# A graph network on one core: edge chunks dealt by degree, sums scattered to DRAM in node order, counts added in DRAM cells

## What is computed

```python
# graph attention, used twice: 8 heads, then 1 head
fs = x @ Ws + bs;  fd = x @ Wd + bd
e = leaky_relu(fs[src] + fd[dst], 0.2)
logits = einsum('ehd,hd->eh', e, attn)
alpha = softmax of logits over the edges of one dst
out = elu(segment_sum(alpha * fs[src], dst))
# whole network
h = relu(ln(x));  h = ln(gat8(h) + h);  x = x + ln(gat1(h))
h = relu(ln(x))
# relational layer: mean over the edges of one type into a node
h1 = sum_r mean_r(h)[n] @ W_rel[r] + h @ W_root + b
# convolution with counts of edges
out = segment_sum(xw[src] * dinv[src] * dinv[dst], dst) + xw * dinv**2 + b,  xw = h1 @ W_gcn
x = x + out
```

## Time and profile before

| what | value |
|---|---|
| runs | 3333.24 us median of 3 (3331.61 to 3335.16) |
| span of the profiled execution | 3343.9 us, 10.7 over that median |
| busy: PE, DVE, ACT, POOL | 2854.4, 2290.3, 1702.4, 1620.6 us |
| same, share of the span | 85%, 68%, 51%, 48% |
| DMA | 546.00 MB, mean 163 GB/s |

### The profile page before, as it was taken

The page is one execution under the profiler, slowest core; times in us unless marked ns, Lnnn a source line. Parts: engine busy times, 40 slices in busy tenths (PEclk is TensorE's granted clock), DMA queues, the critical chain, the costliest instruction groups (busy, mean ns, idle before and its releaser), DMA issues. The chain is left out here.

```text
span 3343.9 us, 59649 instructions
## 1 busy us (share of the span) xinstructions
PE 2854.4 (85%) x13556; PEld 2139.5 (64%) x13557; DVE 2290.3 (68%) x4351; ACT 1702.4 (51%) x5372; POOL 1620.6 (48%) x2067
## 2 busy tenths in 40 slices
PE   5885888888789799998668999999999976777799
PEld 3442454454455455554348999999999974555598
DVE  6535889889767788887565555555555447888743
ACT  0004889899722133332545566555665566777300
POOL 4666566565446555554114545544544445555201
PEclk9897999999999899999789999999999998999899
DMA  4235344444511555555228777777776747666412
GB/s 141 84 81 159 121 135 126 124 134 124 170 46 44 157 167 170 171 170 175 89 95 263 243 242 245 242 237 237 247 241 219 222 144 230 203 210 208 119 34 65
DMA packets 175008, 546.00 MB, mean 163 GB/s; under 512 B 55331, under 2 KB 56343, under 8 KB 174723
## 3 DMA queue, kind: packets, MB, share of 16 engines
q0 software_dynamic: 82000, 370.33, 35.3%
q1 hardware_dynamic: 70596, 122.50, 11.8%
q10 hardware_dynamic: 22304, 52.11, 5.4%
HBM read 461.31 MB, written 83.81 MB: 163 GB/s over the span
## 5 line engine op out<-in xcount | busy, mean ns | idle before, releaser
L2189 PE MATMUL pO<-wh,gT 128*128 128x384 f32 x3264 | 867.1, 339 | 17.6 <-ACT gT L2140 15.6
L805 POOL DMA_INDIRECT row<-fs_d,rec x400 | 455.9, 1140 | 389.6 <-PE pA L1330 157.5
L2189 PEld LDWEIGHTS pO<-wh,gT 128*128 128x128 f32 x3264 | 594.4, 189 | 26.4 <-ACT gT L2140 23.0
L2189 PE MATMUL pO<-wl,gT 128*128 128x384 f32 x1632 | 547.5, 335 | 0.0
L2203 DVE TENSOR_SCALAR cntge<-pT 128x768 int32<-128x768 int32 x137 | 131.2, 958 | 427.2 <-ACT gT L2140 223.1
L1038 ACT ACTIVATE sj<-sj 128x96 f32<-128x96 f32 x1176 | 312.9, 268 | 78.7 <-DVE sj L1155 78.5
L2189 PEld LDWEIGHTS pO<-wl,gT 128*128 128x128 f32 x1632 | 308.3, 189 | 0.0
L2140 ACT ACTIVATE gT<-cntge 128x256 fp32r<-128x256 f32 x822 | 292.9, 410 | 28.1 <-DVE cntge L2206 4.0
L805 POOL DMA_INDIRECT row<-y_d,rec x200 | 204.1, 1020 | 171.6 <-PE pR L2335 113.5
L1077 PE MATMUL pS<-row,ident 128*128 128x384 f32 x400 | 176.2, 524 | 128.3 <-DVE sj L1155 80.9
L2335 PE MATMUL pR<-row,share 128*128 128x384 f32 x384 | 165.7, 582 | 120.6 <-issue 65.0
(11 more groups left out here) (386 smaller groups left out, 5983.8 us busy)
## 6 DMA issues: line engine op xcount, KB each, us to landing
fdt<-in_L_gnn_W_rel_dram SPq DMA_DIRECT2D x170, 384.0 KB
startrow<-seen_d ACTq DMA_DIRECT2D x141, 320.0 KB
raw<-in_L_gnn_W_rel_dram SPq DMA_DIRECT2D x34, 384.0 KB
row<-fs_d,rec POOLq DMA_INDIRECT x400
kept_d<-fdt SPq DMA_DIRECT2D x10, 384.0 KB
kept<-kept_d SPq DMA_DIRECT2D x10, 384.0 KB
fs_d<-of SPq DMA_DIRECT2D x9, 388.0 KB
fd_d<-of SPq DMA_DIRECT2D x9, 388.0 KB
```

What stands on the lines that cost most here:

```text
L805: pool.indirect_dma_start(b["row"][u][:, j, :].bitcast(words), None, table, bass.IndirectOffsetOnAxis(ap=b["rec"][u][:, 2 * j + field:2 * ...
L2189: last = pe.matmul(pO[:, q, 0:HALF], gT[:, c, half, :].bitcast(F32R), w[:, c, lo:up].bitcast(F32R), start=c == 0 and k == 0, stop=c == KC ...
```

## The change

- Nodes are dealt to the 128 partitions in a serpentine by degree rank. Each partition has a stream of chunks of four edges, its nodes one behind another; a group is the next chunk of every stream. 44 groups (11 turns) hold all chunks of these inputs. DVE makes 16 words for each of 64 groups in one block (row of records, node, edges left, target, whether first or last chunk), and SP stores them; the packed table of tiles and `sum_tiles` are gone, as are `perm`, `permc` and `degr`.
- A group's destination row is gathered by POOL with its four source rows (`own_of`). Running sums are in a ring of four slots, `sum0` to `sum3`. POOL scatters each group's sums to `first_d`, `second_d` or `ysum_d` in node order (`sums_out`); partitions whose chunk is not the node's last have a target of NP or above, which the bounds check drops. Before a slot's target is overwritten, `sum_free` waits for the scatter that used it last. The scatter of group u - 1 is issued behind the fetches of group u + 2.
- The joins load and store tiles in node order by SP. In the first join SP also clears `counts_d` (21 stores) and `ge_d`'s first column. Single attention stores each group's comparison with the types to `ge_d`.
- In the second join POOL works out the weights of all edges of 48 groups (EARLY = 48) in eight parts of six groups, writes them into the group words, and does one further group in a loop that also counts its edges.
- In the relation stage POOL adds ones into the cells of `counts_d` with three accumulating scatters (`tally`) in each of 64 pairs (COUNTED = 64), each waiting for the one before.
- The y stage has no comparisons, transposes or counts: ACT makes two shares from the words, PE multiplies two rows, DVE adds. The convolution loads sums and counts from DRAM; its last store is SP's.

The core of the diff:

```diff
-        groups_d = dram("groups_d", (MAX_TURNS * U + U - 1, P, S * 2), I32)
+        groups_d = dram("groups_d", (P, GROUPS, WORDS), I32)
...
+        first_d = dram("first_d", (2 * NP, W), F32)
+        second_d = dram("second_d", (2 * NP, W2), F32)
+        ysum_d = dram("ysum_d", (2 * NP, D), F32)
+        ge_d = dram("ge_d", (P, 1 + GROUPS, S * (RELS + 1)), BF16)
+        rcnt_d = dram("rcnt_d", (NP, RELS), F32)
+        counts_d = dram("counts_d", ((1 + NP) * NP, 1), F32)
...
+                    v.link(dve.tensor_tensor_scan(chunk_end[:], chunks[:], chunks[:], 0.0, ALU.add, ALU.max))
...
+                    with dve.Fori(0, blocks) as k:
+                        w = Steps(dve, dve_step, k * BLOCK_STEPS + v.base)
+                        w.wait()
+                        w.link(dve.tensor_tensor(begun[:], over(grow[:], 2, shape), over(chunk_from[:], 1, shape), ALU.is_ge))
+                        for f in range(5):
+                            w.link(dve.tensor_tensor(part[:], begun[:], over(rise[:, f, :], 1, shape), ALU.mult))
+                            w.link(dve.tensor_reduce(now[:, f, :], part[:], X, ALU.add))
...
+        def sum_free(eng, b, i, off):
+
+            eng.wait_ge(b["sum_out"][off % U], i * 16 + 16 * (off // U + (off % U == U - 1)))
+
+        def open_sums(pool, b):
+
+            pool.iota(b["to"][U - 1][:], [[1, 1]], base=NP, channel_multiplier=1,
+                      allow_small_or_imprecise_dtypes=True).then_inc(b["to_ok"][U - 1], 1)
+            pool.wait_ge(b["to_ok"][U - 1], 1)
+
+        def keep_target(pool, b, i, off):
+
+            u = off % U
+            sum_free(pool, b, i, off)
+            n = off // U + 1 + (u == U - 1)
+            pool.sem_inc(b["posted"], 1)
+            pool.tensor_copy(b["to"][u][:], word(b, u, R_OUT)).then_inc(b["to_ok"][u], 1)
+            pool.wait_ge(b["to_ok"][u], i + n)
+            pool.sem_inc(b["posted"], 1)
+
+        def sums_out(pool, b, off, table):
+
+            u = off % U
+            pool.indirect_dma_start(table, bass.IndirectOffsetOnAxis(ap=b["to"][u][:], axis=0), b["sum"][u][:], None,
+                                    bounds_check=NP - 1, oob_is_err=False).then_inc(b["sum_out"][u], 16)
...
+            def fetch(i, off):
+                u = off % U
+                pool.wait_ge(b["edges_only"][(u - 1) % U], i * 16 + 16 * ((off - 1) // U + 1))
+                rec_wait(pool, b, i, off)
+                pool.sem_inc(b["posted"], 1)
+                pool.tensor_scalar(edge[:], slot[:].rearrange("p s c -> p (s c)"), word(b, u, R_LEFT, F32), None, ALU.is_lt)\
+                    .then_inc(b["edge_ok"], 1)
+                pool.wait_ge(b["edge_ok"], i * U + (off + 1))
+                pool.sem_inc(b["posted"], 1)
+                edges_only(u)
+                keep_target(pool, b, i, off)
+                pool.wait_ge(b["edges_only"][u], i * 16 + 16 * (off // U + 1))
+                pool.sem_inc(b["posted"], 1)
+                used.wait(pool, i, off - U)
+                pool.sem_inc(b["posted"], 1)
+                rows_of(pool, b, u, table, 0, F32)
+                own_of(pool, b, u, own)
...
+                    record(w % U)
+                    fetch(i, u + ROWS_AHEAD)
+                    for s in done:
+                        s.wait(pool, i, u - 1)
                     pool.sem_inc(b["posted"], 1)
-                    v.wait()
-                    edges_only(w % U)
...
+        def gather_rows(pool, b, table, field, own, out_table, readers, done, words=F32):
+
+            open_sums(pool, b)
+
+            def fetch(i, off):
+                u = off % U
+                rec_wait(pool, b, i, off)
+                pool.sem_inc(b["posted"], 1)
+                keep_target(pool, b, i, off)
+                for used in readers:
+                    used.wait(pool, i, off - U)
+                pool.sem_inc(b["posted"], 1)
+                if own is not None:
+                    own_of(pool, b, u, own)
                 rows_of(pool, b, u, table, field, words)
+
+            for off in range(ROWS_AHEAD):
+                fetch(0, off)
             turns = turns_of(pool)
             with pool.Fori(0, turns) as i:
                 for u in range(U):
-                    w = u + ROWS_AHEAD
-                    pool.wait_ge(b["rec_in"][w % U], i * 16 + 16 * (w // U + 1))
-                    for used in readers:
-                        used.wait(pool, i, w - U)
+                    fetch(i, u + ROWS_AHEAD)
+                    for s in done:
+                        s.wait(pool, i, u - 1)
                     pool.sem_inc(b["posted"], 1)
-                    rows_of(pool, b, w % U, table, field, words)
+                    sums_out(pool, b, u - 1, out_table)
...
-                        def keep(i, off, tile):
-                            total.wait(act, i, off)
-                            act.activation(split(of(acc, tile)), halves(pA[off % 2]), ACT.Copy).then_inc(kept.sem, 1)
+                        def keep(i, off):
+                            whole.wait(act, i, off)
+                            sum_free(act, b, i, off)
+                            act.activation(split(total[off % U][:, 0:D]), halves(pA[off % 2]), ACT.Copy).then_inc(kept.sem, 1)
...
+                        def weigh(v, groups, weight):
+
+                            ge, rel = cge[:, 0:groups], crel[:, 0:groups]
+                            of_node = crow[:, 0:groups, :].unsqueeze(2).to_broadcast([P, groups, S, RELS])
+                            v.link(pool.tensor_tensor(rel, ge[:, :, :, 0:RELS], ge[:, :, :, 1:RELS + 1], ALU.subtract))
+                            v.link(pool.tensor_tensor(rel, rel, of_node, ALU.mult))
+                            n = RELS
+                            while n > 2:
+                                half = n // 2
+                                v.link(pool.tensor_tensor(rel[:, :, :, 0:half], rel[:, :, :, 0:half], rel[:, :, :, n - half:n], ALU.add))
+                                n -= half
...
+                        pool.wait_ge(rec_in, 16)
+                        v = Steps(pool, pool_step)
+                        of_edges(v, EARLY, crec[:], cells[:].rearrange("p (g s) -> p g s", s=S))
+                        pool.wait_ge(rcnt_out, 16)
+                        for part in range(EARLY // PART):
+                            at = part * PART
+                            pool.dma_start(cge[:].rearrange("p g s r -> p g (s r)"), ge_d[:, 1 + at:1 + at + PART, :]).then_inc(cge_in, 16)
+                            for g in range(PART):
+                                pool.indirect_dma_start(crow[:, g, :], None, rcnt_d, bass.IndirectOffsetOnAxis(
+                                    ap=crec[:, at + g, R_NODE:R_NODE + 1], axis=0)).then_inc(crow_in, 16)
+                            pool.wait_ge(crow_in, 16 * (at + PART))
+                            pool.wait_ge(cge_in, 16 * (part + 1))
+                            weigh(v, PART, cweight[:, at:at + PART, :])
+                        pool.dma_start(groups_d[:, 0:EARLY, R_WEIGHT:R_WEIGHT + S].bitcast(F32), cweight[:]).then_inc(weight_out, 16)
...
+                                pool.indirect_dma_start(counts_d, bass.IndirectOffsetOnAxis(ap=ccell[:, j:j + 1], axis=0),
+                                                        ones[:, 0:1], None, compute_op=ALU.add).then_inc(counted, 16)
+                                pool.wait_ge(counted, k * (16 * S) + 16 * (j + 1))
...
+                    def tally(out, j):
+
+                        pool.wait_ge(counted, out * (16 * PER_PAIR) + 16 * j)
+                        pool.sem_inc(posted, 1)
+                        pool.indirect_dma_start(counts_d, bass.IndirectOffsetOnAxis(ap=cindex[:, j:j + 1], axis=0),
+                                                ones[:, 0:1], None, compute_op=ALU.add).then_inc(counted, 16)
+
+                    def pair(v, i, n, out, counting=False):
+
+                        if counting:
+                            pool.wait_ge(counted, out * (16 * PER_PAIR))
+                            pool.sem_inc(posted, 1)
+                            v.link(pool.tensor_copy(cindex[:], cells[:, ds(out * PER_PAIR, PER_PAIR)]))
                         for b in range(PAIR):
                             make_list(v, i, n, b + PAIR)
+                            if counting:
+                                tally(out, 2 * b)
                             t_ok.wait(pool, n, b)
                             pool.sem_inc(posted, 1)
                             fetch(b)
                             if out is not None:
                                 put(v, out, n, b - PAIR)
+                            if counting and b == 0:
+                                tally(out, 1)
 
                     v = Steps(pool, pool_step)
...
+                            dve.scalar_tensor_tensor(out=split(total[u][:]), in0=split(total[(u - 1) % U][:]),
```

(48 more changed lines are left out.)

1080 lines of the change are left out of this document (538 added, 542 removed).

## The result

The changed kernel takes 4121.77 us (median of four, 4110.01 to 4122.28) against 3332.43 of the kernel before: 1.236 times as long, interval 1.234 to 1.238, 789 us slower. The forecast was 3621, with a range that ended at 3790. The side was right, the size was not: the forecast was +288, and +789 was measured.

A forecast was written before the change was run, and what follows sets the result against it. PE was taken to fill most of single attention and the relation stage; in the changed edge stages POOL's chain governs. Terms 4 - 40 + 3 + 108 + 55 + 120 + 38 = +288 gave 3621 us, range 3355 to 3790.

The forecast's parts named there:

- the one fact: Edge stages: POOL's chain per iteration becomes scatter, landing, copy, fetch, because running sums are scattered to DRAM.
- the loop of two groups: Attentions: POOL alternates between two groups; summed steps give 26.4 us in first attention, 25.4 in single attention.
- rival of hidden waits: Whole kernel: fetches two groups ahead and idle time hide POOL's longer chain; -130 us, 3203; chance 0.16.
- only POOL's own work: Whole kernel: landings hide in the edge stages, but weights and tallies cost as forecast; +35 us, 3368; chance 0.18.
- queueing rival: Scatters queue behind rows: landings 3.7 to 5 us, uncovered tally waits +40; +153 us, 3774; chance 0.14.
- Relations, +120: Relation stage: copy and three accumulating scatters raise POOL's pair from 14.28 to 16.2 us; +120 us (0 to +230).
- The landing, 2.0 us: Edge stages: a scatter takes 2.0 us to land, with 0 and 3.7 kept for the range.
- Single attention, +108: Single attention: exposed landing makes 12.7 us a group against PE's 9.1; +108 us (-37 to +150).
- First attention, -40: First attention: start 19 us shorter, 44 groups at 13.2 us against 48 at 12.6; -40 us (-75 to +10).
- Second join, +55: Second join: POOL's eight weight parts, store and serial extra group end at 205 to 210 us against 155; +55 (+10 to +100).
- The recorded +73: Second join: alternative using the skill page's twice-slower two-input GpSimd work, tree 2.3 us a part more; total 3639.
- Y stage, +38: Y stage: POOL's chain of scatter, landing, copy and rows takes 9.4 us a group; +38 us (-50 to +108).

The follow-up runs named there:

- late target: Changed kernel with the target index copied, after its landing wait, behind the row fetches instead of ahead in all edge stages; 3939.6 us against 4122.
- two groups behind: On top of the late target, the scatter of group u-2 instead of u-1 is issued; 3772.2 us, timed again 3763.36, 1.129 times the kernel before.

## Why the prediction was wrong

*What bounds it, and the one fact.* Right. The order scatter, landing, copy, fetch is what sets the y stage and, through the loop of two groups, both attentions. The late target and the two groups behind show it on both sides: 182 and then 167 us. The rival of hidden waits fell; so did that of only POOL's own work. The queueing rival had landings of 3.7 to 5 us; they were 2.3 and 2.6 on the mean, so it fell too in the edge stages, but its waits between tallies came, at 96 us for its 40.

*Relations, +120: the step that failed most,* 230 of the 501 us by which the forecast was short. The term was 11.5 + 4.7 = 16.2 us a pair. Plain scatters without waits give 16.6, of which POOL still waits 1.1 for ACT (69.7 us in the stage), so this much was sized well. Two things were wrong. I priced an accumulating scatter by the marks and the y store, which are plain: it issues in 1.62 us, not 1.1. And I called the waits between tallies covered because a fetch or a list stands between them; at a landing of 4.4 us a list of 2.4 us covers half. Form and waits together are 200 us. The upper end of the term had the waits at 1.7 a pair and no dearer scatter, and so lay at +230 where +350 came.

*The landing, 2.0 us.* Nearly right, though read off one small scatter at the start. It was 2.3 us on the mean in single attention, between 1.3 and 5.3, and 2.6 in the y stage. The 3.7 of the row gather, which I kept as the upper end, was the worse guess.

*Single attention, +108, came +188.* The period is 13.9 instead of 12.6 (43 periods, +55; the loop's own 12.7 would have given 5 us more). The term that failed in the loop is PE's passes, which I priced at 0.33 us from a stage where PE runs without a hole and the clock is 0.98. I had PE starve for 3.5 us a group and did not ask what its passes cost after that. In the round above they took 2.4 us more than that price, and the landings of the scatter and of the rows 0.9 more. And start and end of the stage together grew by 27 us, which I had left unchanged. The last scatter is such an end:

```profile
1843.69 1.00 POOL L884 DMA_INDIRECT second_d<-sum,to  x1 [12.88 <-ACT sum L1372]
...
1855.00 0.38 SPq L1835 DMA_DIRECT2D rden<-second_d  x1
```

From 1844.7 to 1855.0 all engines wait for it, 10.3 us, where in the kernel before the last copy to SBUF was 1.1 us from the next stage. The forecast charged 3 us for this in first attention and nothing here.

*First attention, -40, came +80.* The loop was right in its parts, but 13.2 was the sum of parts at their shortest: 15.5 came, 97 us over 43 periods. PE's 16 passes of sums took 6.9 us (619.22 to 626.09, at a granted clock of 0.50 to begin with, after a wait of 8.2 us) instead of 5.3, and about 7 in most groups. POOL's scatter took 1.5 to 1.7 instead of 1.0, and its index copy 2.0 to the next fetch (637.08 to 639.09) instead of 1.1. The start gave 13 of the 19 us I had booked, and the end cost 19 instead of 3.

*Second join, +55, came +76.* The weights began 27.5 us into the stage for 20 and took 152 us for 142, the store 15 for 15, the extra group 35 us for 28, with four scatters at about 6. Within the weights two misses cancel in part, the tree 3.0 us a part too low and the landing 1.7 too high. The two-input operations on 816 elements took 1.76 us, 2.2 ns an element against DVE's 1.24 at 0.95 per 768. The Trainium skill's page GPSIMD Engine Reference, Engine selection, has about twice for two inputs; the trace, with 1.7 times, roughly agrees. By that factor on DVE's row the 2424 elements would take 6.0 us, an estimate, against the 6.5 above. The recorded +73 came near +76 in part by luck: it doubled POOL's own price for writing, and the late start and the extra group made up for the rest.

*Y stage, +38, came +78.* 10.0 a group for 9.4, which is the landing's 0.6 (+26), the rest at the ends.

*Projection, first join and convolution* were right within 5 us each; in the first join, with the 21 clearing stores in it, no more than 3 us were lost.

*The range.* Its upper end, 3790, was the queueing rival with a little more, so it held only what that rival held: it had no dearer scatter, no lower clock and no longer ends of stages, which all add. The store of 6144 pieces, a term that no row bounded, was right at 15 by luck. Even the sum of the upper ends of all stages, +619, would not have held the result, as the relation stage and both attentions each passed their own.

## What to carry to other kernels

A wait for the landing of a scatter cost 1.6 us a group in single attention and 2.3 in the y stage while it stood ahead of the fetches, and moving it behind them gave that back: put the reuse of a small index behind the next work, and let stores trail the loop by two steps instead of one. Where a forecast has TensorE starve in every round, do not price its passes at the clock of a stage without holes. When running sums move out of SBUF, count each step that the engine which issues the transfers now takes in the loop, and count the last landing of every stage. An accumulating transfer has a price of its own; measure one before 192 are put on the path.

## What the runs showed of the hardware that was not expected

- An accumulating indirect scatter of 128 single words took 1.62 us to issue (median of 192) against 1.02 for the same without addition. In the relation stage both were waited for until late, 4.4 us (with addition) and 5.0 us (plain) after the issue in the median of the waits. With little else on the queue the adding one took 4.2 to 4.6; a small plain one at the start took 2.0, but no run has a plain one in the same place.
- After a wait of 5.29 us PE ran its first passes at a granted clock of 0.50, after one of 1.19 us at 1.00; over the steady part of single attention the clock was 0.86 with holes of 2 to 7 us before two of three groups, and 0.99 with holes of about 1 us.
- A single store of 6144 pieces of 16 bytes took 2.3 us to issue and another 13.1 until POOL's next transfer.
- Two-input elementwise operations on GpSimd took 2.2 ns an element of 128 partitions, 1.7 times DVE's.
